# Flamingo block: first batch of x loaded and normed tile by tile, Wq in two column halves

## The reference, cut to what matters

```
xn  = layernorm(x)                      # over D = 256, eps 1e-5
q   = xn @ Wq                           # Wq: 256 x 1024, 16 heads of 64
kh, vh = ctx @ Wk, ctx @ Wv             # ctx: 2 x 1024 x 256
x   = x + tanh(g) * (softmax(mask(q kh^T / 8)) vh @ Wo + bo)
x   = x + tanh(g2) * moe_ffn(layernorm(x))   # 8 experts, each row goes to its best one
```

## Time and profile before

| | us |
|---|---|
| three runs | 213.63, 215.0, 215.24; median 215.0 |
| the profiled execution, its own time | 213.29 |
| its span, first to last instruction | 211.5 |
| PE busy in the span | 196.0 (93%) |
| DVE, ACT, POOL busy | 126.3, 103.5, 89.3 |
| first matmul of q starts at | 12.06 |
| mean granted clock of TensorE | 0.993 |

### The profile page before, as it was taken

The page is one execution under the profiler, slowest core; times in us unless marked ns, Lnnn a source line. Parts: engine busy times, 40 slices in busy tenths (PEclk is TensorE's granted clock), DMA queues, the critical chain, the costliest instruction groups (busy, mean ns, idle before and its releaser), DMA issues.

```text
span 211.5 us, 4026 instructions
## 1 busy us (share of the span) xinstructions
PE 196.0 (93%) x1284; PEld 144.4 (68%) x1284; DVE 126.3 (60%) x525; ACT 103.5 (49%) x372; POOL 89.3 (42%) x129
## 2 busy tenths in 40 slices
PE   7899989889999999999999789998999999979950
PEld 7753477557767454688895656775788999859940
DVE  0589873799899232154327899989834347265520
ACT  1221532799999321302217699998541254435510
POOL 7000090557577940000000799776930003777460
PEclk9999999999999999999999999999999999999997
DMA  4994188999999200290000011600000000254010
GB/s 112 348 391 170 33 284 294 329 313 326 286 200 342 81 2 0 67 329 0 3 0 2 14 52 38 206 2 0 3 0 2 3 0 25 88 170 137 33 54 21
DMA packets 21185, 25.16 MB, mean 119 GB/s; under 512 B 1875, under 2 KB 19741, under 8 KB 21024
## 3 DMA queue, kind: packets, MB, share of 16 engines
q1 hardware_dynamic: 19136, 22.51, 35.0%
q0 software_dynamic: 1152, 2.12, 3.0%
q10 hardware_dynamic: 864, 0.15, 0.4%
HBM read 14.14 MB, written 11.68 MB: 122 GB/s over the span
## 4 chain that ended last, share of the span: by engine, by line
PE 61%; issue 14%; DVE 7%; DMA 6%; ACT 6%; POOL 3%; POOLq 0%; DVEq 0%; ACTq 0%
PE s_bank L1580 13%; PE o_bank L1663 7%; PE t_bank L1637 7%; PE o_bank L1537 7%; PE s_bank L1620 6%; PE s_bank L1689 4%; ACT probs L768 4%; PE o_bank L1656 4%; PE s_bank L1880 3%; DMA rows<-in_x_dram 3%; PE o_bank L1891 2%; DMA oT<-sorted_rows 2%; PE t_bank L1671 2%; DVE probs L1225 1%; DVE pT L1246 1%
## 5 line engine op out<-in xcount | busy, mean ns | idle before, releaser
L608 POOL TENSOR_TENSOR probs<-probs,r_col 128x512 f32<-128x512 f32 x32 | 33.4, 1043 | 62.1 <-DVE r_col L1236 61.7
L768 ACT ACTIVATE probs<-probs,negm_run 128x160 f32<-128x160 f32 x128 | 53.0, 416 | 5.2 <-DVE negm_run L1225 5.0
L1225 DVE CUSTOM_DVE_ANT_0 probs<-s_bank,maskneg 128x160 f32<-128x160 f32 x128 | 33.1, 318 | 5.8 <-PE s_bank L1620 5.5
L1580 PE MATMUL s_bank<-xnT,wq_sb 128*128 128x512 f32 x64 | 28.8, 598 | 0.3 <-ACT xnT L721 0.3
L1537 PE MATMUL o_bank<-wo_sb,oT 128*128 128x256 f32 x128 | 28.6, 379 | 0.0
L1537 PEld LDWEIGHTS o_bank<-wo_sb,oT 128*128 128x128 f32 x128 | 23.9, 190 | 3.5 <-issue 0.5
L768 ACT ACTIVATION_READ_ACCUMULATOR probs<-probs,negm_run 128x1 f32 x128 | 24.0, 187 | 0.0
L1620 PE MATMUL s_bank<-k_sb,q_sb 64*128 64x160 f32 x256 | 22.3, 311 | 0.0
L1620 PEld LDWEIGHTS s_bank<-k_sb,q_sb 64*128 64x128 f32 x256 | 17.9, 186 | 4.8 <-issue 4.0
L1580 PEld LDWEIGHTS s_bank<-xnT,wq_sb 128*128 128x128 f32 x64 | 11.7, 190 | 13.4 <-issue 13.3
L1637 PE MATMUL t_bank<-ident,probs 128*128 128x128 f32 x128 | 18.7, 284 | 1.7 <-issue 1.1
(11 more groups left out here) (150 smaller groups left out, 306.3 us busy)
## 6 DMA issues: line engine op xcount, KB each, us to landing
sorted_rows<-empty_row SPq DMA_DIRECT2D x8, 1040.0 KB, 14.1
oT<-in_L_ffn_W_dram SPq DMA_DIRECT2D x1, 2048.0 KB, 19.0
q_sb<-in_L_ffn_W_dram SPq DMA_DIRECT2D x1, 2048.0 KB, 8.4
oT<-sorted_rows SPq DMA_DIRECT2D x1, 1040.0 KB, 5.3
oT<-sorted_rows SPq DMA_DIRECT2D x8, 130.0 KB, 2.4
rows<-in_x_dram SPq DMA_DIRECT2D x2, 512.0 KB, 8.7
wq_sb<-in_L_xattn_Wq_dram SPq DMA_DIRECT2D x1, 1024.0 KB, 8.6
mask_sb<-in_mask_BxSxS_bk_dram SPq DMA_DIRECT2D x2, 512.0 KB, 10.6
```

The source lines that it names most:

```text
L608: nc.gpsimd.tensor_tensor(window_wide(u), window_wide(u), r.rearrange("p i h -> p (i h)") .unsqueeze(2).broadcast_to([P, 4, WIDE]), ALU.mu ...
L768: last = nc.scalar.activation(window_part(u, i, h), window_part(u, i, h), ACT.Exp, bias=negm_run[at], scale=-1.0, accum_out=l_run[at])
L1225: nc.vector.tensor_tensor_reduce(window_part(u, i, h), s_bank[u % 2][:, h, i * CK:i * CK + WK], maskneg[:, q, 0:WK], -SCALE, LARGEST, ALU. ...
L1580: last = nc.tensor.matmul(bank[m % 4], wq_sb[:, c, m * P:(m + 1) * P], xnT[:, c, b * N:(b + 1) * N], start=(c == 0), stop=(c == DC - 1))
```

## The change

SP loads x of batch 0 as four DMAs of 128 KB, a semaphore each; Wq as two DMAs of 512 KB (its columns 0 to 511 and 512 to 1023: 2 KB runs in place of 4 KB), with the mask of batch 0 between them; and the mask of batch 1 ahead of x of batch 1. ACT takes four square roots, each behind its tile's variance. DVE takes variance and norm tile by tile, the norm one tile behind the variance. PE runs 9 `keep_busy` matmuls in place of 22 at the start and 2 between one tile's transposes and the next one's; it waits for Wq's first half at the first block and for the second at block 4.

```diff
-            load_x(0)
-            sp.dma_start(wq_sb[:], wq.rearrange("(c p) n -> p c n", p=P)).then_inc(s_wq, 16)
+            def load_wq(half):
+                cols = slice(half * INNER // 2, (half + 1) * INNER // 2)
+                sp.dma_start(wq_sb[:, :, cols], wq.rearrange("(c p) n -> p c n", p=P)[:, :, cols]).then_inc(s_wq[half], 16)
+
+            for q in range(QT):
+                sp.dma_start(x_sb[:, q, :], x[0, q * P:(q + 1) * P, :]).then_inc(s_x_tile[q], 16)
+            load_wq(0)
             load_mask(0)
+            load_wq(1)
             for b in range(1, B):
+                load_mask(b)
                 load_x(b)
-                load_mask(b)
...
-            std1(0)
+            for t in range(QT):
+                act.wait_ge(first_var, t + 1)
+                nc.scalar.activation(std[:, t:t + 1], rows[:, t, VAR:VAR + 1], ACT.Sqrt, bias=eps[:]).then_inc(first_std, 1)
...
-            dve.wait_ge(s_x[0], 16)
-            variance(range(QT))
-            norm(0, QT, xn, ln_ready)
+            def first_variance(t):
+                dve.wait_ge(s_x_tile[t], 16)
+                then(nc.vector.bn_stats(stats[:, t, :], x_sb[:, t, :]))
+                nc.vector.bn_aggr(rows[:, t, MEAN:MEAN + 2], stats[:, t, :]).then_inc(first_var, 1)
+
+            def first_norm(t):
+                dve.wait_ge(first_std, t + 1)
+                then(nc.vector.reciprocal(rows[:, t, RSTD:RSTD + 1], std[:, t:t + 1]))
+                nc.vector.tensor_scalar(xn[:, t, :], x_sb[:, t, :], rows[:, t, MEAN:MEAN + 1], rows[:, t, RSTD:RSTD + 1],
+                                        ALU.subtract, ALU.mult).then_inc(ln_ready, 1)
+
+            first_variance(0)
+            for t in range(1, QT):
+                first_variance(t)
+                first_norm(t - 1)
+            first_norm(QT - 1)
+            dve.sem_inc(var_ready, 1)
...
-            keep_busy(22)
+            keep_busy(9)
             pe.wait_ge(ident_ready, E + 3)
...
                 for i in range(QT):
+                    if i > 0:
+                        keep_busy(between)
                     pe.wait_ge(ln_ready, b * QT + i + 1)
...
-            xn_transposes(0)
+            xn_transposes(0, 2)
             keep_busy(2)
-            pe.wait_ge(s_wq, 16)
+            pe.wait_ge(s_wq[0], 16)
...
+                if b == 0 and m == M // 2:
+                    pe.wait_ge(s_wq[1], 16)
```

More of the change, by code:

```diff
@@ L257, in flamingo_kernel @@
         bank = [pair[:, i] for pair in (s_bank[0], s_bank[1], t_bank, o_bank) for i in range(2)]
-        s_x = [sem(f"s_x{b}") for b in range(B)]
-        s_wq = sem("s_wq")
+        s_x = [None] + [sem(f"s_x{b}") for b in range(1, B)]
+        s_x_tile = [sem(f"s_x_tile{q}") for q in range(QT)]
+        s_wq = [sem(f"s_wq{half}") for half in range(2)]
         s_mask = [sem(f"s_mask{b}") for b in range(B)]
@@ L268, in flamingo_kernel @@
         var_ready = sem("var_ready")
+        first_var = sem("first_var")
+        first_std = sem("first_std")
         std_ready = sem("std_ready")
@@ L1501, in _, with xn_transposes @@
             pe.wait_ge(ident_ready, 2)
-            keep_busy(22)
+            keep_busy(9)
             pe.wait_ge(ident_ready, E + 3)
-            def xn_transposes(b):
+            def xn_transposes(b, between=0):
                 for i in range(QT):
+                    if i > 0:
+                        keep_busy(between)
                     pe.wait_ge(ln_ready, b * QT + i + 1)
```

## The result

| | before | after |
|---|---|---|
| measured together, median (runs) | 214.38 us (213.63 to 215.24; 4) | 212.34 us (211.85 to 212.74; 4) |
| ratio after / before, 95% interval | | 0.9897 [0.9864, 0.993] |
| profiled execution, span | 213.29, 211.5 | 212.74, 210.9 |
| first matmul of q | 12.06 | 11.32 |

Three of the four runs of before are the ones known ahead of the change; the fourth took 213.76. The medians lie 2.0 us apart, and the ratio's middle is 1.03% under one. The two profiles, however, show a difference of only 0.55 us. That gap between profile and median is what most of the experiments are about.

The account below looks back on a forecast made before the run. Before 12.06 us the chain from x's load through DVE and ACT was the bound, not PE. Norms 0.92 us earlier, less 0.3 for keep_busy, taken as 0.7: 215.0 - 0.7 = 214.3; own range 213.5 to 215.1, 8 in 10 213.2 to 216.5.

Parts of the forecast that it names:

- The prediction's own sign of being wrong: Wrong if q starts after 12.06 with quick matmuls, or time moves over 1% while q's start moves under 1 us.
- the sum: Whole kernel: profiled 213.29 minus 0.7 is 212.6; three-run median 215.0 minus 0.7 is 214.3.
- Part 1: Loads of x on SP: four tiles replace one 512 KB wait, landing at 3.5, 4.5, 5.5 and 7.0.
- Part 2: Variance and norm by tile on DVE and ACT: first square root 6.21, last norm 9.88, 0.92 us earlier.
- Part 3: PE transposes with keep_busy between: gives back 0.3 us; q starts 0.7 earlier, at about 11.4.
- rival 1: PE's clock rises only during the transposes or soon after q starts: +0.3 us, 215.3; chance 0.30.
- Part 4: Wq in halves and masks moved: q waits nothing; first mask costs 0, at worst 0.6 us on DVE.
- The fear that nine matmuls endanger the clock: PE's start: nine matmuls end at about 5.2, shorter than the 5.9 us before the quick pace; clock may not have risen.
- Rival 2: PE's clock stays low through the transposes' gaps and rises only inside q: +3.2 us, 218.2; chance 0.08.
- rival 3: Loads of x: tiles land one after another at 2.0 us each; gain 0.4, 214.6; chance 0.08.
- rival 4: PE reaches visit_sums before the masks are reduced and waits there for what it gained: 215.0; chance 0.05.

Follow-up runs that it names:

- b_again: The kernel before, unchanged, measured and profiled once more: 213.8 us, ratio 0.9989.
- a_again: The changed kernel, unchanged, measured and profiled once more: 212.16 us, ratio 0.9915 against the kernel before.
- order_only: The kernel before with only Wq in halves and the masks moved: 214.15 us, ratio 0.9973.
- x_whole: The changed kernel with x of batch 0 loaded by one DMA again: 215.4 us, ratio 1.0064 against the kernel before.
- between0: The changed kernel without keep_busy matmuls between the tiles' transposes: 212.94 us, ratio 0.99 against the kernel before.
- b_look4: The kernel before, unchanged, in a further profile: 215.37 us at a mean clock of 0.983.
- tiles_only: The kernel before with x of batch 0 in four DMAs, DVE still working in batches: 214.32 us, ratio 1.001.
- act_late: The changed kernel with ACT's six small DMAs issued only after its copy of the transposed x: 210.9 us, ratio 0.9827 against the kernel before.
- kb22: The changed kernel with 22 keep_busy matmuls at the start in place of 9: 214.4 us, ratio 0.9979 against the kernel before.

## Why the prediction was wrong

The forecast was 214.3 us, a gain of 0.7, range down to 213.2; measured were 212.34 and a gain of 2.0. The sign was right; the size was off by a factor of three (the ratio's interval is a gain of 0.7 to 1.4%), and the median lies below the whole range. The prediction's own sign of being wrong came: the time moved by over 1% while q's start moved by less than 1 us.

**The step that failed** is the sum: "It lies 1.7 below the median of the three runs, so for a median I take 215.0 - 0.7 = 214.3." It took the distance between profile and median, 1.7 us, as one and the same constant for both kernels. It is not a constant: in the changed kernel the profile took 212.74 and the median is 212.34, a distance of -0.4. The profiled time itself was forecast at 212.6 and came at 212.74, so these 2.1 us are the whole of the miss of 2.0 (214.3 against 212.34). In the kernel before it comes with the landing of x: 7.00 in the profile that I read, 5.6 to 7.6 over six profiles, with q always 5.06 us behind it. Spans of b_again's eleven other runs (211.6 to 213.5) say by the yardstick that q mostly began at 12.0 or later, some with a clock loss of 1.3 on top. The changed kernel has no such spread (its runs are within 0.9 us), so its gain against a typical run of before is larger than against that profile. On a_again's chip the 20 of 29 runs of before with a mean clock above 0.985 have a median of 213.7, 1.6 us above the changed kernel's 212.16, and the 9 others one of 215.3, 3.2 above. The later x is thus the larger part of the gain and the falls of the clock the smaller; for runs without a profile both are read from time and mean clock. A spread of 1.6 us in three runs was before my eyes, and I used it only as noise.

**Profile against profile the forecast of q was right by luck:** 0.74 us earlier, 0.7 forecast. The parts were not:

- Part 1: tiles taken at 3.5, 4.5, 5.5 and 7.0, landed at 3.7, 4.15, 5.8 and 7.5. Good. Tile 3 did bind DVE for 0.46 us, which I had at nothing.
- Part 2: the first square root was taken at 6.21, "bound by ACT, not by x". The reason held, the time was 5.17: ACT's six issues ended 1.0 us earlier. The last norm ended at 9.17, not 9.88.
- Part 3: taken at the quick clock. The profile has rival 1, slow transposes with PE as the bound, 1.28 us a tile as worked out; it started 1.1 us earlier than I had it (6.14 and not 7.2), and the two errors cancelled. In a_again the quick case came, with q at 10.58: the gain there is 1.5 against the first profile, not 0.7.
- Part 4: nothing within what order_only can tell (0.9941 to 1.0006), and Wq and the masks were in time. Block 4 comes 6.3 us behind Wq's second half by the prediction's own figures (18.3 less 12.0), not 3.5.
- Two small slips of the sum: four norms of 0.408 in 1.38 overlap by 0.08 a pair and not 0.06, and 0.92 less 0.3 is 0.6, where 0.7 was taken. Neither changes the outcome.
- The fear that nine matmuls endanger the clock was right in kind (x_whole and between0 show falls), but I charged it to the changed kernel alone. The kernel before pays it too, when x is late behind 22 matmuls that are through: shown in b_look4, and by their mean clock likely in the others of 38 in 97 runs.

Rival 2 (low clock long into q) was not seen in the changed kernel's two profiles (it was in between0's), rival 3 (tiles one after another) is excluded by landings 0.4 to 1.7 us apart, rival 4 by visit_sums, which began 0.75 us behind the end of DVE's mask work (19.22 and 18.47), as it did before (19.95 and 19.19).

The Trainium skill's rule for small transfers ("DMA: Bandwidth & Descriptors", rules for kernel authors) is to coalesce them into one large one. To go against it cost nothing here: by tiles_only four loads of 128 KB in place of one come out the same, 1.001 [0.998, 1.004]. The fixed cost of 2.0 us that the prediction cites stands there for DMAs that GpSimd issues, and these are SP's. In any case it was not paid by each tile in turn: in act_late the tiles landed 0.5, 0.5 and 1.1 us apart.

Left open: why four of six profiles of the kernel before have x earlier than its other runs must have had it, and what exactly the small loads hold up (issue, descriptors or the engines). One hint: of the 97 runs only three have a span under 211 us (212.21, 212.31 and 212.45 us), and each of them stands first in its row of runs, as a profiled run does. Two other rows of before begin with 213.92 and 213.66. A first execution may differ from the later ones; no run tests it.

## What to carry to other kernels

Before a gain is summed against one profile, ask whether the term that is removed is the same in every run: a wait on a first load is not, and runs that spread by more than the gain are a reason to look at their spans and clocks. Removing a wait whose length varies gains its mean, not the value that one profile shows, and makes the kernel steadier. And look at who else is on the queues while the first load is under way: moving six small loads by 8 us gained 3.3 us of median, and splitting the big one with all that came with it 2.0.

## What was unexpected of the hardware

- Six loads of together under 150 KB, issued by ACT beside SP's load of x, delayed x by 1.1 to 3.1 us and differently from run to run (landing 5.6 to 7.6 in six profiles, without them 4.49 in one). With x in tiles ACT's issues ended at 3.64 in after, a_again, tiles_only, between0 and kb22 alike; with x in one load its table load began between 4.0 and 5.3.
- The clock's rise under the same keep_busy stretch from 1.21 came at 4.9 to 5.0 (three times), 5.7, 6.7 and 7.1 us in six profiles of the same kernel, by the pace; so the same 22 matmuls lasted 6.9 to 8.0 us.
- The clock fell after 3.1 us without work (x_whole, 5.2 to 8.3) and after some 2.4 us of idling with 1.3 us of transposes behind it (b_look4), while in a_again gaps of 0.97 and 0.74, with keep_busy between the transposes, left it high. In between0 it fell at 8.0 behind gaps of 1.08 and 0.74 without keep_busy.
